# Two attention layers on one core: PSUM banks named per item, softmax sums by transposes, squares and first loads moved

## The reference

```python
sa = _mha(x, x, swq, sbq, swk, sbk, swv, sbv, swo, sbo, mask, bias)
x = _layernorm(x + sa, g1, be1)
ca = _mha(x, mem, cwq, cbq, cwk, cbk, cwv, cbv, cwo, cbo, None, None)
x = _layernorm(x + ca, g2, be2)
ff = jax.nn.gelu(x @ w1 + b1, approximate=False) @ w2 + b2
return _layernorm(x + ff, g3, be3)
```

## Time and profile before

| | us |
|---|---|
| median of 3 runs (585.9 to 589.45) | 588.11 |
| profiled execution | 583.32 |
| its span, first to last instruction | 581.4 |
| busy PE / DVE / ACT / POOL | 528.0 / 443.4 / 423.0 / 337.9 |

### The profile page before, as it was taken

How to read it: one execution, slowest core, us unless ns; L and a number is a source line. 1 busy time by engine, 2 the same in 40 slices (tenths; PEclk the granted TensorE clock), 3 DMA queues, 4 the chain that set the end, 5 groups by cost and what they waited for, 6 DMA issues and landing times.

```text
span 581.4 us, 17475 instructions
## 1 busy us (share of the span) xinstructions
PE 528.0 (91%) x6868; PEld 289.7 (50%) x6868; DVE 443.4 (76%) x887; ACT 423.0 (73%) x658; POOL 337.9 (58%) x638
## 2 busy tenths in 40 slices
PE   3378998887899999999999999999999999999984
PEld 2246666664444444545454545455555444444432
DVE  5425665557989999888888887878787899999922
ACT  3135556453478787888989898989898888787792
POOL 7334688784464372837385858585858556362022
PEclk9969999998999999999999999999999999999998
DMA  3983455564370724514261605170707081643000
GB/s 102 205 234 116 118 135 144 147 167 127 85 185 4 183 90 96 155 30 132 53 158 29 172 14 165 22 177 10 184 4 183 11 188 47 138 124 54 12 11 20
DMA packets 86116, 61.47 MB, mean 106 GB/s; under 512 B 6462, under 2 KB 85550, under 8 KB 85946
## 3 DMA queue, kind: packets, MB, share of 16 engines
q1 hardware_dynamic: 85536, 60.14, 41.4%
q10 hardware_dynamic: 498, 0.21, 0.1%
HBM read 32.93 MB, written 26.22 MB: 102 GB/s over the span
## 4 chain that ended last, share of the span: by engine, by line
PE 66%; ACT 7%; issue 7%; DVE 6%; SPq 5%; POOL 4%; DMA 4%; ACTq 0%; POOLq 0%; DVEq 0%
PE pv L612 19%; PE dps L593 12%; PE aps L548 10%; ACT probs L743 5%; DVE negmax L890 4%; PE dps L690 4%; DMA kst<-k_parts 3%; PE aps L658 3%; PE dps L707 3%; PE aps L672 3%; PE aps L647 2%; PE dps L695 2%; PE aps L642 2%; PE dps L701 1%; PE dps L575 1%
## 5 line engine op out<-in xcount | busy, mean ns | idle before, releaser
L890 DVE TENSOR_REDUCE negmax<-dps 128x1 f32<-128x512 f32 x512 | 323.6, 684 | 38.3 <-PE dps L593 34.1
L743 ACT ACTIVATE probs<-aps 128x1024 f32<-128x1024 f32 x288 | 283.0, 1026 | 60.3 <-PE aps L548 29.0
L612 PE MATMUL pv<-probs,vp 128*32 128x256 f32 (+1 forms) x3072 | 156.9, 330 | 0.0
L593 PE MATMUL dps<-kst,qst 61*128 61x512 bf16 x512 | 120.3, 385 | 6.0 <-DVE negmax L890 4.2
L548 PE MATMUL aps<-qst,kst 64*128 64x256 bf16 x1024 | 97.4, 272 | 2.1 <-ACT probs L743 0.7
L997 POOL TENSOR_SCALAR mcap<-negmax 128x16 f32<-128x16 f32 x48 | 12.2, 254 | 145.5 <-DVE negmax L890 75.0
L612 PEld LDWEIGHTS pv<-probs,vp 128*32 128x32 f32 x3072 | 69.0, 109 | 55.1 <-issue 28.7
L548 PEld LDWEIGHTS aps<-qst,kst 64*128 64x128 bf16 x1024 | 36.9, 94 | 58.9 <-ACT probs L743 20.6
L593 PEld LDWEIGHTS dps<-kst,qst 61*128 61x128 bf16 x512 | 32.2, 93 | 66.4 <-DVE negmax L890 47.7
L886 DVE TENSOR_REDUCE negmax<-dps 128x4 f32<-128x512 f32 x64 | 41.2, 686 | 21.5 <-PE dps L584 21.5
L930 DVE COPY mT<-dps 24x256 bf16<-24x256 bf16 x48 | 13.1, 273 | 35.5 <-PE dps L701 35.4
(11 more groups left out here) (129 smaller groups left out, 771.6 us busy)
## 6 DMA issues: line engine op xcount, KB each, us to landing
kst<-k_parts SPq DMA_DIRECT2D x64, 192.0 KB, 4.5
qst<-q_parts SPq DMA_DIRECT2D x48, 192.0 KB, 3.8
k_parts<-ks SPq DMA_DIRECT2D x16, 384.0 KB, 2.6
q_parts<-qs SPq DMA_DIRECT2D x24, 192.0 KB, 2.0
cin<-in_ctx_dram SPq DMA_DIRECT2D x16, 256.0 KB, 2.8
k_parts<-ks SPq DMA_DIRECT2D x16, 256.0 KB, 3.0
q_parts<-qs SPq DMA_DIRECT2D x24, 128.0 KB, 2.0
k_parts<-ks SPq DMA_DIRECT2D x24, 128.0 KB, 3.1
```

Source lines behind the costliest of these rows:

```text
L593: mm = nc.tensor.matmul(dve_entry("X", u.index, n + g), q[rows_in(g, 0, ROW_M), four, tile * P:(tile + 1) * P], k[rows_in(g, 0, ROW_M), fo ...
L612: mm = nc.tensor.matmul(pv[32 * j:32 * j + 32, dst:dst + n], vp[u.parity][:, c, 4 * quad + j, :], probs[:, quad, src:src + n], start=(quad ...
L743: nc.scalar.activation(probs[:, quad, part * 1024:(part + 1) * 1024], src, ACT.Exp, scale=SCALE).then_inc(act_emptied, 1)
L890: ins = nc.vector.tensor_reduce(negmax[:, tile, at:at + 1], src, AX.X, ALU.max, negate=True)
```

## The change

1. The two rings become one tensor `ps` of seven banks. Each item in the strings names its banks (`S:01`, `X:45`); a planner (`bank_places`) notes for each entry which entry of ACT and which of DVE used these banks last, and PE waits for these. The strings are new, with the items in another order; H is two halves with a bank each. A third self order and one for step 0 are added.
2. D transposes the four blocks with the identity; `pick` goes. DVE reads sums and values out of the transposed blocks, with two multiplications in place of one.
3. Squares of the context are taken in steps 0 to 7 (item C, one batch each, four squares), from loads of their own into the still unused buffer of the hidden layer. POOL computes all 32 inverse roots at once in step 8. The item `sq` takes the two squares of x.
4. The parts of Q and K go through two DRAM buffers in turn, so the store of unit n waits for the stack loads of unit n-2, not n-1.
5. First loads: at step -1 x of the other batches comes first, then the stores of unit 1, then the copies of constant rows to stack 1. Those to stack 2 are issued by ACT at step 0. The other weights and constants come at step 0, those of the feed-forward part at step 1, the key mask at step 3. The stack loads precede M0's rows in step -1 too. The bias product B moves from step -1 into step 0.
6. Value products of half a quad signal after chunks 1 and 3 each, and wait for the last score tile that they use.

```diff
-CROSS = ("XC S X B3 S X Q X raw K S X P0a S M1 X S D S X P0b S S X P1a X S S sq0 X P1b X V X A S M0 S X O P2a "
-         "sq1 S X S P2b X S S sq2 X P3a X T")
+SELF = "C B3 XC:56 V:0 raw Q:3 S:45 M1:1 D:0 K:1 X:43 S:56 X:21 P0 X:04 S:23 P1 A:5 M0:0 S:34 X:51 O:2 P2"
+CROSS = ("X:45 S:01 X:64 sq XC:23 X:01 S:56 B3 X:42 raw M1:3 S:01 Q:6 X:52 X:43 S:01 K:5 D:2 S:01 X:46 P0a "
+         "S:23 X:10 S:45 P0b X:23 A:6 S:45 S:01 X:26 P1a X:52 S:34 X:60 P1b S:45 X:12 V:6 S:45 X:03 P2a M0:0 "
+         "X:14 S:56 S:23 O:0 P2b S:45 X:61 S:23 P3a T:4")
...
+def bank_places():
+    act, dve, banks, freed, last = {}, {}, {}, {}, {}
...
+            for numbers, key, mine in made:
+                numbers[key] = len(numbers)
+                banks[key] = sorted(mine)
+                freed[key] = tuple(max([n for by, n in map(last.get, mine, [(None, 0)] * 2) if by is engine], default=0)
+                                   for engine in (act, dve))
+                for bank in mine:
+                    last[bank] = numbers, numbers[key] + 1
...
-            def act_entry(*key):
-                at = ACT_AT[key]
-                if at >= ACT_RING:
-                    pe.wait_ge(act_emptied, at - ACT_RING + 1)
-                return aps[:, at % ACT_RING, :]
+            def empty_banks(*key):
+                by_act, by_dve = FREED[key]
+                if by_act > 0:
+                    pe.wait_ge(act_emptied, by_act)
+                if by_dve > 0:
+                    pe.wait_ge(dve_emptied, by_dve)
+                return banks_of(*key)
...
-                            at = (2 * t + r) * 72
-                            mm = nc.tensor.matmul(dst[:, at:at + 72], raw[:, r * LQ + t * P:r * LQ + (t + 1) * P],
-                                                  pick[:, :], start=True, stop=True)
+                            mm = nc.tensor.transpose(dst[:, (2 * t + r) * P:(2 * t + r + 1) * P],
+                                                     raw[:, r * LQ + t * P:r * LQ + (t + 1) * P], ident[:, :])
...
+            def square_context(batch):
+                act.wait_ge(early_loaded[batch % 2], 16 * (batch // 2 + 1))
+                for c in range(CT_N):
+                    if batch * CT_N + c > 0:
+                        act.wait_ge(context_summed, batch * CT_N + c)
+                    nc.scalar.activation(nsq[:, :], in_hidden[batch % 2][:, c, :], ACT.Square,
+                                         accum_out=csum[:, batch, c:c + 1]).then_inc(context_summed, 1)
...
             def store_q(n):
-                if n.index > 0:
-                    sp.wait_ge(stacks_loaded, STACK_LOADS * n.index)
-                    sp.wait_ge(stacks_rest, 32 * n.index)
+                if n.index > 1:
+                    sp.wait_ge(stacks_loaded, STACK_LOADS * (n.index - 1))
+                    sp.wait_ge(stacks_rest, 32 * (n.index - 1))
```

More of the change, by code:

```diff
@@ L128, in all_items @@
         tile = pair = 0
-        for name in self.order().split():
+        for token in order_of(self.i).split():
+            name, _, banks = token.partition(":")
+            at = tuple(int(bank) for bank in banks)
             if name == "S":
-                yield "scores", self.main, tile
+                yield "scores", self.main, tile, at
                 tile += 1
             elif name == "X":
-                yield "maxima", self.nxt, pair
+                yield "maxima", self.nxt, pair, at
@@ L135, in all_items @@
                 pair += 1
             elif name == "raw":
-                yield "raw", self.before, None
-            elif name in SQUARES_OF:
+                yield "raw", self.before, None, at
+            elif name == "sq":
                 far = self.far
-                yield "squares", far if far is not None and far.stage == 2 else None, SQUARES_OF[name]
+                yield "squares", far if far is not None and far.stage == 2 else None, None, at
+            elif name == "C":
+                yield "context", self.main, None, at
@@ L160, in ring_places @@
             elif kind == "maxima":
[L161 to L171, removed]
+                made = [(dve, ("X", u.index, 2 * what + g), at[g:g + 1]) for g in range(2)]
+            elif what == "H":
+                made = [(act, ("H", u.index, half), at[half:half + 1]) for half in range(2)]
+            elif kind in ("act", "dve"):
+                made = [(act if kind == "act" else dve, (what, u.index), at[:1] if u.stage == 0 else at)]
+            else:
+                made = []
@@ L360, in copy_rows, with banks_of @@
                               ).then_inc(stack_rows[i], 16)
+        def banks_of(*key):
+            first, last = BANKS[key][0], BANKS[key][-1]
+            return ps[:, first, :] if first == last else ps[:, first:last + 1:last - first, :]
         block = ctx.enter_context(nc.Block())
@@ L711, in _ @@
             for s in STEPS:
-                for kind, u, what in s.items:
+                for kind, u, what, _ in s.items:
                     if kind == "scores":
@@ L790, in take @@
                         act.wait_ge(dve_filled, DVE_AT["F", u.index - 1] + 1)
[L791 to L794 removed]
+                    else:
+                        act.wait_ge(context_summed, B * CT_N)
+                    for half in range(2):
+                        src = entry("H", u.index, half)
+                        for f in (2 * half, 2 * half + 1):
+                            ins = nc.scalar.activation(hT[:, f, :], src[:, f % 2 * LQ:f % 2 * LQ + LQ], ACT.Gelu,
+                                                       bias=cols[:, 6 + f:7 + f])
+                        ins.then_inc(act_emptied, 1)
             def copy_raw(u):
@@ L962, in _ @@
             for s in STEPS:
-                if s.i == 1:
+                if s.i == 2:
                     make_key_mask()
-                for kind, u, what in s.items:
+                for kind, u, what, _ in s.items:
                     if kind == "maxima":
```

275 lines of the change are left out of this document (152 added, 123 removed).

## The result

| | before | after |
|---|---|---|
| median of 4 runs each, same chip | 588.78 us (585.90 to 589.54) | 571.58 us (569.88 to 575.24) |
| profiled execution, its span | 583.3 us, 581.4 us | 571.68 us, 569.9 us |

The ratio after to before is 0.9751, 95% interval 0.9707 to 0.9796: 15 us gained by the ratio, 17 by the medians, 11.5 between the two profiled spans. The forecast had 26.5 less than the profiled 583.3, that is 556.8; measured were 571.7.

The account below looks back on a forecast made before the run. TensorE (PE), 91% busy, was taken as the bound, standing because of fixed bank rings. 12.8 + 4.2 + 4.5 + 3.0 + 1.0 + 1.0 = 26.5 us off 583.3 gives 556.8, 561 as median; range 552 to 571, chance 0.60.

Parts of the forecast that it names:

- the rival in which only the work that is gone counts: Whole kernel: PE's standing moves to other banks, or later K lengthens self steps 2 us; 12.7 us gained, 575; chance 0.18.
- D at half its 1.04: D's block on PE: transposes cost 0.5 us instead of 1.04, saving 0.54 us of PE per step, 24 times.
- the rival in which they don't overlap: D's transposes cost 273 ns each, so D saves nothing in 18 steps, about 9 us less gain: 570; chance 0.05.
- Feed-forward steps: Eight cross steps with feed-forward: 1.6 us less each (1.1 standing, 0.5 D), to 27.0 us; 12.8 us in all.
- The standing of 1.7 us: PE idle per 28.56 us feed-forward step, blamed on the fixed bank rings; 1.1 us of it taken as gone.
- worth nothing in the cross steps by the equal 28.56 us: Moving context squares off ScalarE in cross steps: no gain, as steps lasted 28.56 us with no squares or six.
- Plain steps: Six plain cross steps: 0.7 us less each, 24.30 to about 23.6, VectorE the next limit; 4.2 us in all.
- The slower rival: First scores of a step wait for M0's late rows, up to 2.6 us in 14 steps: 598; chance 0.07.
- The start: New order of first loads: M0's rows at 26.8, first scores at 30.5 to 31 instead of 35.32; 4.5 us gained.
- the constants: Their loads return in step 0: four issues, 1.8 us, ahead of unit 2's stores, which wait for POOL anyway; no cost.
- Self steps: D's 0.5 us comes through in six self steps, 12.89 to 12.4 us, later K mostly filling slack; 3.0 us in all.
- Hand-over: Steps 7 and 8, between self and cross steps: 1.0 us gained.

Follow-up runs that it names:

- k_early_self: Kernel after with Q and K right behind XC in the self steps and the context squares later: 575.90 us, ratio 0.9811 to the kernel before.
- d_products: Kernel after with D as products with `pick` again instead of transposes: 580.65 us, ratio 0.9888 to the kernel before.
- squares_back: Kernel after with four more squares per cross step at item `sq`, their sums unread: 581.69 us, ratio 0.9923 to the kernel before.
- rings: Kernel after, same new order of items, but each bank taken from the old rotating rings: 615.26 us, ratio 1.0477 to the kernel before.
- best: Kernel after with Q and K early in step 7, a smaller first x load, M0 and POOL's part earlier in late plain steps: 575.75 us, ratio 0.982.
- m0_first: Kernel after with M0's rows loaded ahead of unit 1's stack loads in step -1: 570.32 us, ratio 0.9722 to the kernel before.
- one_buffer: Kernel after with one DRAM buffer each for the parts of Q and K, with the old wait: 572.25 us, ratio 0.9756 to the kernel before.
- no_context: Kernel after with the context squares and their loads left out, their sums set to 1: 570.11 us, ratio 0.9729 to the kernel before.
- k_early_last: Kernel after with Q and K early in the last self step (step 7) alone: 570.81 us, ratio 0.9738 to the kernel before.
- c_late: Kernel after with the context squares moved from the start to the end of the self steps: 571.52 us, ratio 0.9747 to the kernel before.

## Why the forecast was right, and which of its terms weren't

**Faster, by the later half of the kernel, at the upper edge of what was given.** The median of 571.6 is 0.6 us above the range of 552 to 571 that had 0.60, and inside 543 to 582. It is 10.6 above the 561 forecast and nearer to the 575 of the rival in which only the work that is gone counts; of 26.5 us 11.5 to 17 came, by which of the three measures one takes. But it didn't come about that rival's way: its steps of 28.0 us are out (27.36), and so are its self steps made longer by the later K (k_early_self). Behind unit 10 the forecast's terms hold: 14.4 of 16.6 us. D at half its 1.04 is right (0.44 us), but it is worth 0.41 in the step and not 0.54, since in the new order the products would take 0.84 (d_products). The clue was the chain of XC's four transposes, not their 273 ns each; the rival in which they don't overlap is out.

**Feed-forward steps, 27.36 instead of 27.0.** A steady step gained 1.1 to 1.2 us, not 1.6: 0.4 by D (d_products), which leaves 0.7 to 0.8 for the standing where 1.1 was taken. The standing of 1.7 us was read too large. Of the 1.96 us on ScalarE I gave PE only the 16 value products; its timeline before shows eight score products and two for the maxima in the same time, and no idle time:

```profile
284.75 1.07 PE L612 MATMUL pv<-probs,vp 128*32 128x256 f32 x16
285.75 0.39 PE L548 MATMUL aps<-qst,kst 64*128 64x256 bf16 x4
285.98 0.38 PE L593 MATMUL dps<-kst,qst 61*128 61x512 bf16 x2
```

The argument "worth nothing in the cross steps by the equal 28.56 us" doesn't carry over either: it was read off the old order. squares_back shows that four more squares cost 1.34 us a step in the new one, as much as the whole gain, when they stand in one row with the two of x; spread as before they may cost less. The edits don't add up. D alone gives 0 in a cross step and 0.4 with the rest; the order without its banks is 3.0 us worse than with them (rings); with order, banks and D, but the six squares in one row, a step is 0.1 to 0.3 longer than before. I had named ScalarE as standing "less in the way of score tiles" and counted that in the 1.1, so how those 0.7 to 0.8 us split between banks and squares is not shown.

**Plain steps, 23.3 to 23.6 as forecast.** VectorE is busy 22.31 of 23.56 us. But D was counted as nothing there, since VectorE was the limit, and d_products shows it worth 0.26 us a step: some of PE's work lies on the path of these steps too.

**The slower rival appeared, and was cheap.** It asked for the first scores of a step to wait for M0's rows. They do, in the chain of a plain step after:

```profile
492.30 0.69 DVE negmax L945
492.99 0.51 SPq L485
...
493.55 3.47 DMA qst<-mT
...
497.06 0.41 PE ps L582 x4
```

M0 stands late in the order, the rows land at 497.0 and PE waits 0.6 us for them (0.9 its weight load). The rival's condition was 1.9 us. The landing took 3.47 where I had 2, but there was no backlog: M0's copy began at 491.97, right behind its product, with none of the maxima of later tiles ahead of it. With M0 and POOL's part for it earlier (best) a plain step was 0.8 to 1.0 us longer.

**The start gave 2.0 us instead of 4.5.** SP's queue at the start, timeline (start, us, engine and line, DMA):

```profile
17.01 2.00 SPq L433 DMA_DIRECT2D q_parts<-qs  x3
19.05 1.88 SPq L441 DMA_DIRECT2D k_parts<-ks  x3
...
26.41 2.09 SPq L466 DMA_DIRECT2D qst<-q_parts  x2
28.55 1.93 SPq L472 DMA_DIRECT2D kst<-k_parts  x4
30.52 1.51 SPq L485 DMA_DIRECT2D qst<-mT  x2
```

M0's rows were due at 26.8 in my sum and were issued at 30.52. Stores took 3.9 (I had 3), the copies landed 2.7 after the last was issued (1.5), the stack loads took 4.1 (2.7): three terms too small by 3.5 together. m0_first shows that changing places gives nothing, not even where the first scores come 2.4 us earlier.

**And the constants cost 4.2 us in step 0, costed at nothing.** I followed their DMA issues (1.8 us, "ahead of unit 2's stores, but these wait for POOL anyway") and not what is computed from them. In the kernel before, VectorE prepared the derived weights from 28.07 to 29.5 us and PE made `wo` times `bvb` ahead of the first scores, both idle then. After, timeline of VectorE and PE:

```profile
44.47 1.29 DVE L941 TENSOR_REDUCE negmax<-ps 128x4 f32<-128x512 f32 x2 [0.29 <-PE ps L618]
...
46.53 0.47 DVE L922 TENSOR_SCALAR bvb<-zero,cols 128x128 f32<-128x128 f32 x2
...
47.16 0.68 PE L721 MATMUL ps<-wo,bvb 128*128 128x128 f32 x4 [2.14 <-DVE bvb L922]
```

PE stands 2.1 us for them. Another 0.9 goes where the first K (moved behind X) has its banks emptied by ScalarE (`PE ps L564 <- ACT ks L805`, 0.9 us). The clock shows the rest of the tale without settling it: 0.50 from 33.28 to 42 us, its lower level of 1.2 GHz, as before from 30 to 40 (before, from 34 to 42, it was 0.59). The constants alone weren't put back, so the split of the 4.2 us is read from waits and not shown by a run.

**Self steps: the term of 3.0 us came to -0.1.** In no kernel with these self steps did it pass 1.9 (squares_back). Where nothing disturbs them they take 12.1 to 12.3 us in nearly every variant, better than the 12.4 forecast. In the kernel after, `raw` 1 came 14.42 after `raw` 0 (before: 13.23) and `raw` 3 came 13.63 after `raw` 2. SP's queue is the cause that I can show for a part of the first: in step 0 it is one unbroken chain from 34.99 to 50.80 us (M0's rows, constants, context loads, stores, stack loads), and PE waits for what it loads last. From the chain of waits:

```profile
42.68 2.47 SPq L441
...
50.85 2.54 DMA kst<-k_parts
...
53.43 0.41 PE ps L609 x4
```

That wait is 0.8 us of PE in the step of 14.42 us. The rest of it, 1.3 us, and the loss in the other are in the section on the hardware.

**Hand-over, -0.9 instead of +1.0.** In step 7 the stack loads of unit 9 go out behind M0's rows, at 150.21 and 151.20 us, and land late: the chain goes over them until 157.57. PE stands in short pieces, the longest for VectorE's maxima (0.83 us before 160.74), and its clock follows. From the chain, and then two stretches of 4 us, the clock third from last:

```profile
151.71 5.86 DMA kst<-k_parts
...
162.94 1.86 PE pv L646 x16
```

```profile
160.00:164.00 4.00, 3.26 (x27) 1.31 (x31) 4.00 (x9) 2.25 (x3) 2.22 (x4) 0.83 0.01 2
164.00:168.00 4.00, 4.00 (x28) 1.53 (x20) 3.06 (x7) 1.74 (x3) 0.00 (x0) 0.74 0.58 179
```

The block of 16 value products at 162.94 takes 1.86 us instead of 1.00; from 163.0 to 165.5 the granted clock is 0.50, the lower level. Step 8 is 29.28 us against 25.74 before; steps 6 and 7 together are 2.7 us shorter. An earlier K in the last self step gave back 0.2 (its step 8 took 27.7 us, where 26 was expected), while kernels with edits elsewhere took 65.4 (one_buffer) to 68.1 us (no_context), so that 0.2 is nothing. Step 8 was 27.7 us in these two as well, still 2 above the 25.74 before. What would mend it stays open.

## What to carry to other kernels

An edit that is worth nothing in a step can be worth something once its neighbours are in (D: 0, then 0.4 us of 27.4): read "no difference" as "hidden by what bounds it now", and ask again after each change, with the edit taken out of the new kernel rather than put into the old one. An order of work and the buffers it is written for are one thing: here the new order in the old rings was slower than both kernels, and so was the old order with banks given out by a simple rule. When a load is moved, follow everything computed from it to its new place, on every engine, and not the issue of the load alone.

## What the runs showed of the hardware that I had not expected

**Stops inside a block of products.** In self steps of the kernel after, PE stops for 1.3 to 1.5 us in the midst of a block of value products that wait for nothing the profile shows. Timeline of PE, two of them:

```profile
58.64 0.42 PE L646 MATMUL pv<-probs,vp 128*32 128x64 f32 x14 [1.30 <-issue]
...
85.47 0.31 PE L646 MATMUL pv<-probs,vp 128*32 128x64 f32 x6 [1.47 <-issue]
```

The kernel before has none over 1 us in its self steps. The steps of 12.1 us have none, and 13.63 less 1.47 is 12.16. So these stops are the second loss of the self steps. The first of them recurs in step 1 of eight variants, after the same 18 products with 14 to go: 1.2 to 1.5 us in k_early_last, m0_first, one_buffer, rings and squares_back, 0.5 to 1.0 in no_context, c_late and k_early_self, at other times in each (58.25 in k_early_last). So it belongs to a place in the program and not to a moment. The DMA engines are busy 0.54 of the stretch around the second. Why PE stops there is not shown.

**One power over 32 columns** took 5.46 us on POOL (L1070), where 6 columns take 1352 ns; it was bounded by 7.2 and lies beside other work:

```profile
L1070 POOL TENSOR_TENSOR crs<-cms,minushalf 128x32 f32<-128x32 f32 x1 | 5.5, 5455 | 0.1
```

**Four transposes of 128x128 fp32 cost 0.44 us of chain where four products of 72 columns with weights of the same size cost 0.84 to 1.04**, at 273 and 281 ns by their own rows. The Trainium skill ("TensorE: Matmul & The Clock Gate", Part 4: PE-mode transpose) gives about 275 ns for a transpose in a kernel, beside a figure for bf16; the trace agrees with that as a duration for fp32, and the chain shows that it isn't what one of four costs.
